# Where a transformer block turns its tiles: attention heads, second LayerNorm and four x tiles by DMA, with the x loads, one head's plan and the projection's banks rearranged

## The reference, cut to what matters

```python
x = x + attn(layernorm(x))      # x: (4, 2048, 2048) f32
x = x + ffn(layernorm(x))
# attn: 16 heads of 128; lat = rmsnorm(x @ wkv_a.T) (512 wide)
kv = lat @ wkv_b.T;  q = x @ wq.T;  # the last 64 of each head's 128 are rotated
attn = softmax(causal(q k^T / sqrt(128)));  o = (attn @ v) @ out_w.T + out_b
# ffn, width 6144, weights rounded to fp8:
down( silu(gate(x) * gate_scale) * up(x) * up_scale ) * down_scale
```

## Time and profile before

| | |
|---|---|
| time, median of 3 runs | 1630.77 us (1630.75 to 1630.99) |
| the profiled execution: time, span of its slowest core | 1630.0 us, 1628.2 us |
| TensorE matmul busy | 1573.4 us (97%) |
| VectorE, ScalarE, GpSimd busy | 449.1, 390.1, 87.4 us |
| mean granted TensorE clock, all cores | 0.995 to 0.997 |

### The profile page before, as it was taken

One profiled execution on the slowest core, in us unless ns is written; L12 is line 12 of the kernel. 1 busy time (PEld: TensorE's weight loads), 2 busy tenths in 40 slices (PEclk: granted clock), 3 DMA queues, 4 the chain that ended last, 5 costly groups with the idle time before them and its releaser, 6 DMA issues.

```text
span 1628.2 us, 23216 instructions; the slowest of 8 cores (1626.8 to 1628.2 us)
## 1 busy us (share of the span) xinstructions
PE 1573.4 (97%) x8897; PEld 780.2 (48%) x9034; DVE 449.1 (28%) x1002; ACT 390.1 (24%) x529; POOL 87.4 (5%) x160
## 2 busy tenths in 40 slices
PE   4798999999999999999999999999999999999998
PEld 3543555555555444444444444444444444444444
DVE  5754444444455663110111111111111011111111
ACT  4543666666664111111111001111111000000000
POOL 0310010000000000000000000000000000000000
PEclk9999999999999999999999999999999999999999
DMA  9822454121137942535555664664353293939210
GB/s 300 249 48 42 72 75 70 31 34 24 28 56 127 220 120 104 50 28 47 45 45 47 54 51 39 52 49 42 33 46 26 18 113 51 108 70 117 66 54 28
DMA packets 33098, 117.14 MB, mean 72 GB/s; under 512 B 3744, under 2 KB 6112, under 8 KB 28128
## 3 DMA queue, kind: packets, MB, share of 16 engines
q0 software_dynamic: 17856, 58.73, 36.4%
q1 hardware_dynamic: 15136, 56.93, 10.9%
HBM read 233.08 MB, written 16.78 MB: 153 GB/s over the span
## 4 chain that ended last, share of the span: by engine, by line
PE 93%; DVE 2%; DMA 2%; issue 2%; ACT 1%; SPq 0%; DVEq 0%; POOL 0%; ACTq 0%; POOLq 0%
PE PS L1142 20%; PE PS L1122 20%; PE PS L1128 20%; PE PS L947 7%; PE PS L1104 6%; PE PS L1034 4%; PE PS L1010 4%; PE PS L956 3%; PE PS L966 3%; PE PS L911 2%; DMA X<-xq 2%; PE PS L892 1%; PE PS L991 1%; PE PS L975 1%; DVE BNSa L563 0%
## 5 line engine op out<-in xcount | busy, mean ns | idle before, releaser
L1122 PE MATMUL PS<-X2T,W 128*128 128x512 bf16 x1506 | 344.9, 379 | 2.6 <-DVE RES L701 1.1
L1128 PE MATMUL PS<-X2T,W 128*128 128x512 bf16 x1505 | 344.9, 379 | 1.6
L1122 PEld LDWEIGHTS PS<-X2T,W 128*128 128x128 fp8e4 x1536 | 150.1, 98 | 182.3 <-issue 1.5
L1128 PEld LDWEIGHTS PS<-X2T,W 128*128 128x128 fp8e4 x1536 | 150.3, 98 | 181.2
L755 DVE SCALAR_TENSOR_TENSOR FUSE<-PS,CF,SIL 128x512 bf16<-128x512 f32 x96 | 72.0, 750 | 589.9 <-PE PS L1128 581.3
L877 ACT ACTIVATE SIL<-PS,CF 128x512 bf16<-128x512 f32 x96 | 65.9, 687 | 584.7 <-PE PS L1122 584.7
L829 ACT ACTIVATE P<-PS,NEGB 128x1024 bf16<-128x1024 f32 x192 | 170.2, 900 | 81.5 <-PE PS L1010 74.1
L1142 PE MATMUL PS<-WDa,FUSE 128*128 128x512 fp8e4 x768 | 166.1, 379 | 1.2 <-DVE FUSE L755 1.2
L1142 PE MATMUL PS<-WDb,FUSE 128*128 128x512 fp8e4 x768 | 166.1, 379 | 0.0
L1142 PEld LDWEIGHTS PS<-WDa,FUSE 128*128 128x128 bf16 x768 | 75.0, 98 | 92.1 <-issue 1.6
L1142 PEld LDWEIGHTS PS<-WDb,FUSE 128*128 128x128 bf16 x768 | 75.2, 98 | 90.6
(11 more groups left out here) (130 smaller groups left out, 1050.9 us busy)
## 6 DMA issues: line engine op xcount, KB each, us to landing
W<-gu POOLq DMA_DIRECT2D x48, 512.0 KB, 10.2
X<-xq SPq DMA_DIRECT2D x8, 1024.0 KB, 15.1
X<-xo SPq DMA_DIRECT2D x8, 1024.0 KB, 8.5
WQ<-wq POOLq DMA_DIRECT2D x16, 512.0 KB, 6.7
WO<-wo POOLq DMA_DIRECT2D x16, 512.0 KB, 11.1
RES<-xq SPq DMA_DIRECT2D x8, 1024.0 KB, 13.5
res_scr<-RES SPq DMA_DIRECT2D x8, 1024.0 KB, 6.0
RB<-res_scr SPq DMA_DIRECT2D x32, 256.0 KB, 5.0
```

The source lines that it names most:

```text
L1122: mm = e.matmul(bank(2 * (f % 3)), W8[io % 4][:, c * 128:(c + 1) * 128], X2T[:, c * 1024 + qb * 512:c * 1024 + qb * 512 + 512], start=(c = ...
L1128: mm = e.matmul(bank(2 * (f % 3) + 1), W8[io % 4][:, 2048 + c * 128:2048 + (c + 1) * 128], X2T[:, c * 1024 + qb * 512:c * 1024 + qb * 512 ...
```

## The change

32 turns of heads (O), 8 turns of the second LayerNorm and 4 turns of tiles 12 to 15 leave TensorE and ScalarE. SP issues a DMA that transposes each: `dma_start_transpose` from ON to OT, XH2 to X2T, and XH12 to XH15 to one tile XOTL. Tiles 0 to 11 are still turned by TensorE. SP's list of loads changes: tile 0 in two halves, x tiles 3, 4 and 5 each one place ahead of a latent weight. VectorE's statistics and TensorE's first `lat` calls are reordered. Head 0 has a plan of its own, `STEPS_0`. The projection's banks rotate, the first feed-forward items use other banks, and the down product waits for fewer feed-forward results at first. Cut to its core:

```diff
+STEPS_0 = ["q16 K0:7", "", "", "K1:6 K2:7", "V0:6 K3:7", "q16", "", "N:7", ...]
 STEPS_V = [
     "K0:7",
     "q16",
-    "O1:7",
+    "",
...
-                            + [(10, 0, 12, 4), (11, 1, 12, 4)]):
+                            + [(10, 0, 12, 3), (11, 1, 12, 3)]):
...
+XOTL = at("XOTL", 8192, BF16, o_vb1)
...
     def out_bank(t, d):
-        return 6 + d % 2 if t == 0 else d
+        return (6, 7, 0, 1)[d] if t == 0 else (2 + d) % 4
+
+    def ffn_bank(f):
+        return 2 * ((f + 2) % 3)
...   # sync_prog
+        for n in range(12, 16):
+            e.wait_ge(v_xh, n + 1)
+            e.dma_start_transpose(out=A(XOTL, (n - 12) * 128, [[8192, 128], [512, 16], [1, 128]]),
+                                  in_=XH[n - 12][:, :]).then_inc(d_late[n - 12], 16)
...
+        def turn_heads(h, qb):
+            e.wait_ge(v_on, 4 * h + 2 * qb + 2)
+            e.dma_start_transpose(out=A(OT, h * 1024 + qb * 512, [[16384, 128], [128, 4], [1, 128]]),
+                                  in_=ON[qb][:, :]).then_inc(d_heads[qb], 16)
...
         for t in range(8):
             e.wait_ge(v_add, 4 * (t + 1))
+            e.dma_start(out=res_d.ap()[t * 128:(t + 1) * 128, :], in_=RES[t % 4][:, :]).then_inc(d_spill[t % 4], 16)
+            e.wait_ge(v_xh, 16 + t + 1)
+            e.dma_start_transpose(out=A(X2T, t * 128, [[16384, 128], [1024, 16], [1, 128]]),
+                                  in_=XH2[t % 2][:, :]).then_inc(d_turn[t % 2], 16)
...   # vector_prog
-            if n < 6:
+            if n < 3:
                 stats(n)
-            if 5 <= n < 15:
+            if n in (2, 3):
+                stats(n + 1)
+            if 5 <= n < 8:
+                stats(n)
+            if 7 <= n < 15:
                 stats(n + 1)
             normalise(n)
...
             if bk == 0 and h > 0:
-                e.wait_ge(t_o, count(("O", h - 1, qb)))
+                e.wait_ge(d_heads[qb], 16 * h)
...   # tensor_prog
+            elif dl == 0:
+                for i in range(4):
+                    e.wait_ge(d_late[i], 16)
...
                 if lo == 0 and d == 0:
-                    e.wait_ge(s_o, 29)
+                    e.wait_ge(d_heads[0], 240)
                 for c in range(lo, lo + n):
                     if d == 0 and c == 15:
-                        e.wait_ge(s_o, 31)
+                        e.wait_ge(d_heads[0], 256)
...
             if f == 0:
+                for i in range(2):
+                    e.wait_ge(d_turn[i], 32)
+            if f == 1:
                 e.wait_ge(v_add, 32)
             if f == 2:
-                e.wait_ge(s_t, 48)
-            if f < 2:
-                e.wait_ge(s_t, 40)
+                for i in range(2):
+                    e.wait_ge(d_turn[i], 64)
...
-        e.wait_ge(v_fuse, 96)
+        e.wait_ge(v_fuse, 92)
```

More of the change, by code:

```diff
@@ L19 @@
 VW = 130
+STEPS_0 = [
+    "q16 K0:7",
+    "",
+    "",
+    "K1:6 K2:7",
+    "V0:6 K3:7",
+    "q16",
+    "",
+    "N:7",
+    "X:6 V1:7",
+    "Y:6",
+    "V2:7",
+    "V3:6",
+]
 STEPS_V = [
@@ L49 @@
     "",
-    "Y:6 O0:7",
+    "Y:6",
     "",
@@ L82, in head_plan @@
     at = 0
-    for s, line in enumerate((STEPS_V if h < 12 else STEPS_N) if h < 15 else []):
+    for s, line in enumerate(STEPS_0 if h == 0 else STEPS_V if h < 12 else STEPS_N if h < 15 else []):
         for word in line.split():
@@ L285, in build_nc @@
     d_dsc = sem("d_dsc")
+    d_first = [sem("d_first0"), sem("d_first1")]
+    d_late = [sem(f"d_late{i}") for i in range(4)]
+    d_heads = [sem("d_heads0"), sem("d_heads1")]
+    d_turn = [sem("d_turn0"), sem("d_turn1")]
     d_wkva = [sem(f"d_wkva{i}") for i in range(4)]
@@ L427, in load_wkva @@
             e.dma_start(out=WST[dl][:, :], in_=wkva_d.ap()[dl, :, :]).then_inc(d_wkva[dl], 16)
-        load_x(0)
+        for half in range(2):
+            e.dma_start(out=X[0][:, half * 1024:(half + 1) * 1024],
+                        in_=xq_d.ap()[0:128, half * 1024:(half + 1) * 1024]).then_inc(d_first[half], 16)
         e.dma_start(out=CB[:, :], in_=cb_d.ap()[:, :]).then_inc(d_idb, 16)
@@ L992, in work @@
                                   WO[c][:, d * 512:(d + 1) * 512], start=(c == 0), stop=(c == 15))
-            else:
-                _, h, qb = job
-                e.wait_ge(v_on, 4 * h + 2 * qb + 2)
-                for i in range(4):
-                    mm = e.matmul(bankb(b)[:, i * 128:(i + 1) * 128], ON[qb][:, i * 128:(i + 1) * 128], IDB,
-                                  is_transpose=True, start=(i == 0), stop=(i == 3))
             if last:
@@ L1090, in tensor_prog @@
         values(191)
-        work(("P", 0, 2), 0, 16)
-        work(("P", 0, 3), 0, 16)
-        work(("O", 15, 1), 0, 4)
-        for t in range(1, 8):
+        work(("P", 0, 0), 15, 1)
+        work(("P", 0, 1), 15, 1)
+        for t in range(8):
             for d in range(4):
-                if t == 1:
+                if t == 0 and d < 2:
+                    continue
+                if t == 0:
+                    e.wait_ge(s_exp, 191)
+                elif t == 1 and d < 2:
                     e.wait_ge(s_exp, 192)
@@ L1121, in tensor_prog @@
             for c in range(16):
-                mm = e.matmul(bank(2 * (f % 3)), W8[io % 4][:, c * 128:(c + 1) * 128],
+                mm = e.matmul(bank(ffn_bank(f)), W8[io % 4][:, c * 128:(c + 1) * 128],
                               X2T[:, c * 1024 + qb * 512:c * 1024 + qb * 512 + 512], start=(c == 0), stop=(c == 15))
```

192 lines of the change are left out of this document (94 added, 98 removed).

## The result

The changed kernel takes **1618.24 us** (median of four executions) against 1630.88 for the kernel before on the same chip: ratio 0.9919, 95% interval 0.9896 to 0.9941. It is faster, as forecast, but by 12.6 us and not by 27.6. One of the four (1725.88) and one of before (1867.3) were disturbed; the ratios leave such executions out, and so do all medians from here on, by which after takes 1617.97 and before 1630.77. Measured again in a later series it took 1618.32 (0.9926, 0.9912 to 0.994).

A forecast was written before the change was run, and what follows sets the result against it. TensorE, 93% of the chain of waits, was taken as the bound. Gains of 29.5 us less 1.9 lost at block 3 gave 27.6, so 1603 us; 1596 to 1622 was to hold about 8 in 10.

The forecast's parts named there:

- the landing of the heads' turns: Heads: each 128 KB turn lands in about 3 us, hidden; the tightest, head 15's first half, has 10 us.
- SP's other copies of this size land in 3 to 6 us: Argument against the rival that turns are slower than TensorE's pace and the kernel slower overall; that rival had 0.15.
- SP has nothing else to do there but two residual loads: At head 15: SP's queue holds only these loads, behind turns of heads 14 and 15, needed a tile later.
- The heads' term: Heads: 32 turns leaving TensorE at 0.22 us each give 7.0 us, as heads run without gaps.
- Heads give nothing back: Rival, heads: emptied steps make TensorE wait for ScalarE, so the 7.0 us become waits: 1610 us; chance 0.08.
- The start: First loads and products: reordering gets tile 7 normalised 1.5 us sooner and gains 3.5 us, between 0 and 7.
- the turns of tiles 12 to 15: Before block 3: four turns give 3.6 us, K's wait 1.3; landings of 6.0 us cost a 1.9 us wait.
- head 0: Head 0's start: gaps around the first exponentials and Q's low clock go, net 4.0 us, between 0 and 5.7.
- the projection: First product with WO to feed-forward: 8.7 us gained, including seven tile turns (6.2) and the last add's wait (1.05).
- the feed-forward: From the feed-forward to the end: 2.1 us gained, including the down product's wait of 1.2 us.
- the rival of late turns: Rival: 512 KB turns land in 9 to 12 us each, TensorE waits at block 3: 1614 to 1629; chance 0.12.

The follow-up runs named there:

- e2: Changed kernel, but GpSimd issues the last four output-projection weight loads only after the turn of head 14's first half has landed: 1611.18 us.
- e12: Changed kernel, but the first four feed-forward weight loads go out singly, each after one more projection tile's turn has landed: 1615.02 us.
- e3: Changed kernel with the 32 turns of heads back on TensorE and ScalarE, all else as changed: 1610.62 us.
- e4: Changed kernel with the old start (loads, statistics, first products as before), tiles 12 to 15 still turned by DMA: 1618.52 us.
- e11: e9 with the old start put back as well, tiles 12 to 15 still turned by DMA: 1619.33 us, executions scattered.
- e13: e12 plus the edit of e2 and, in heads 0 to 11, values moved into the emptied step and norms a step earlier: 1606.44 us.
- e6: Changed kernel, but the first four feed-forward weight loads go out only after all four residual tiles have landed: 1618.07 us, executions scattered.
- e9: e6 plus the edit of e2 and, in heads 0 to 11, the emptied step filled with values and norms earlier: 1624.12 us, executions scattered.

## Why the prediction was wrong

- **The step that failed** is the landing of the heads' turns: "The tightest is the first half of head 15 ... That leaves 10 us, and 3 us are hidden." Two things in it were false. The tightest turn is the first half of head 14, read by the first product with WO, since one wait covers the whole bank. And 3 us held for the median turn but not for the one issued 2.9 us behind 2 MB of weights: 14.88, where 7.4 were left. (The half of head 15 that the forecast feared landed in 2.44.) The weight loads of GpSimd were in the trace of before, and I had counted what stands ahead of a turn in SyncE's queue but not in the other one. It cost 6.8 us (e2). A sign of it was on record: "SP's other copies of this size land in 3 to 6 us" looked at stores alone. The same list has the loads of the residual tiles, and on core 6 of before the two issued 3.6 us behind these very weights took 13.8 and 19.7 us:

```profile
RES<-xq SPq DMA_DIRECT2D x8, 1024.0 KB, 13.5
```

- **The residual tiles.** "SP has nothing else to do there but two residual loads" overlooked the same for the second burst: 3.3 us (e12). The tile that came too late stood in SyncE's queue behind a turn that took 30.4 us. In before, loads of residual tiles behind the same burst took 15.5 and 31.9 us on core 6, and TensorE waited for none.
- **The heads' term was mis-sized**: 7.0 us. "The heads run without gaps, so 32 turns give 7.0 us" takes a lack of gaps for a lack of slack. One turn of two stood in the 2.0 us that VectorE takes from Q to the squares, and gave nothing; in heads 12 to 14 neither gave anything. Measured 2.4 us up to the first product (e2 against e3; forecast 6.4), and 1.5 more with the step refilled (340.14 to 338.59). "Heads give nothing back" had 0.08; the truth lay between it and the sum.
- **The start** was mis-sized: 3.5 forecast, 0.4 to 1.0 us on the median core, nothing on the last one. I had tile 7 normalised 1.5 us sooner; on core 6 it ends at 55.92 in place of 54.13 (over the cores 53.6 to 56.0, before 53.6 to 54.7). The reciprocal deviation isn't to blame: up to 56 us VectorE waits 5.3 us for it in all, and waited 5.8. But it waits longer for x tiles to land, 10.8 to 11.8 us (medians over the cores, eleven profiles) against 10.3 to 10.6 with the old start (before, e4, e11). So the tiles do not come sooner in sum; why not, stays open.
- **Right**: the turns of tiles 12 to 15, even better (4.6 for 3.0). They landed in 4.3 us, so the forecast's 1.9 us of waiting did not come. The Trainium skill's page Advanced Engine Details and Errata, section X-Bar Transpose (TRN2), says that transposing DMAs are as fast as regular ones. This row agrees, 4.3 us against the 3.9 of a plain copy that I had worked out. Beside loads the same size took 10.3 us in the projection (the median of XHa), but plain transfers are slower there too, and no run compares the two.
- **Right**: head 0 (4.7 for 4.0, full clock), the projection (9.5 for 8.7 once the bursts are out of the way; tiles 13.8 us apart) and the feed-forward (2.1 to 2.5 for 2.1).
- **Missed in kind**: the rival of late turns looked for a slow turn everywhere, and never for a single late one. The medians of the turns were fast enough everywhere; one turn of 14.88 us, where TensorE had 7.4 left, cost the most.

Without the bursts and with the step filled the sum is 25.9 us by stretches and 24.0 by the medians (1630.41 - 1606.44). The forecast of 1603 described, but for nearly half of the heads' turns and most of the start, the kernel of e13. That its 27.6 us come this close is partly luck: head 0, tiles 12 to 15 and the projection gave 3.1 us more than forecast, while heads and start gave 5.2 less.

## What to carry to other kernels

Before a copy on an engine is replaced by a DMA, list for every one of these DMAs what *other* queues issue in the few microseconds ahead of it; the price is set by the one that stands behind a burst of loads, not by the median. Space a burst out, or hold it behind the transfer that is urgent; moving it whole only changes its victim. And work taken off a busy engine is worth nothing where it stood in the shadow of a latency: compare the distance from the producer's end to the consumer's start before and after, and put other work into the step that it leaves.

## What was unexpected of the hardware

- A transposing DMA is dear to *issue* when loads are in flight: SyncE's queue was held 1.2 us for a head's 128 KB and 1.3 to 3 us for 512 KB with little beside it, 3 to 10 us with a residual load or a weight load beside it, and 21 to 42 us for one turn on every core behind four 512 KB weight loads (e3, e6, e9). The issue of a plain load took 0.3 to 0.9 us even behind the burst of after. A merged row of SyncE can hide a wait, so a long one is to be checked against its list of waits.
- The page counts 46128 packets under 512 bytes where before had 3744; the 42384 more are the turns' 10.5 MB in pieces of some 250 bytes. By these counts a head's turn is about 42384 / 80 = 530 packets, and four weight loads, at 58.73 MB in 17856 packets for that queue, are about 640, though they carry 16 times the bytes (both are estimates; whether the engines take turns by the packets that the profile counts is not shown). The Trainium skill's page DMA: Bandwidth & Descriptors, section Queues, rings and completion order, says that each DMA engine goes round its queues packet by packet; the turn that landed at 492.5 us, within half a microsecond of the last of the four loads (issued at 476.3, 16.0 us to landing), fits that, but no run here separates it from other causes.
- How the two queues share the engines when SyncE stands still for 42 us stays open. The four weight loads suffer as well: on core 0 of e9 they landed 39 to 58 us after their issue, on core 3, where the burst began ahead of the turn, after 11 to 28.
